# A fused attention and FFN block on one core: another order of the setup work, lighter filler matmuls, and one GpSimd copy moved into the loop

## The reference

```
xn  = layernorm(x)                                # no scale, no shift
qkv = xn @ w_qkv.T + b_qkv                        # per head q, k, v
att = softmax(causal(q k^T / 4 + bias[i - j]))    # position bias per head
a   = (att @ v) @ w_proj.T + b_proj
f   = bf16(fp8(xn) @ fp8(ffn_w)) + ffn_b          # in bf16, two scalar scales
out = x + a + f
```

## Time and profile before

| | |
|---|---|
| median of 3 runs | 779.12 us |
| the 3 runs | 775.78, 779.69, 779.12 us |
| profiled execution, its own time | 775.78 us |
| its span, first to last instruction | 774.0 us |
| mean granted TensorE clock | 0.994 |

### The profile page before, as it was taken

How to read it: one execution, slowest core, us unless ns; L and a number is a source line. 1 busy time by engine, 2 the same in 40 slices (tenths; PEclk the granted TensorE clock), 3 DMA queues, 4 the chain that set the end, 5 groups by cost and what they waited for, 6 DMA issues and landing times.

```text
span 774.0 us, 23381 instructions
## 1 busy us (share of the span) xinstructions
PE 745.4 (96%) x6413; PEld 503.3 (65%) x6413; DVE 634.2 (82%) x2399; ACT 581.6 (75%) x1263; POOL 531.3 (69%) x525
## 2 busy tenths in 40 slices
PE   7989999999999999999999999999999999999997
PEld 4666566666766667676666767666676766667555
DVE  4898798888889888888988888898888889878723
ACT  4457888787788878778877877887787787877672
POOL 8345767686776768776776777677687767767581
PEclk9999999999999999999999999999999999999999
DMA  6432344435334433533543353344335334433301
GB/s 180 178 138 91 121 174 153 126 117 180 121 128 173 151 126 117 182 124 123 173 151 126 118 183 125 119 173 151 129 119 182 127 115 172 152 109 118 120 32 62
DMA packets 55313, 105.67 MB, mean 137 GB/s; under 512 B 10420, under 2 KB 30388, under 8 KB 55284
## 3 DMA queue, kind: packets, MB, share of 16 engines
q1 hardware_dynamic: 53968, 104.52, 37.9%
q10 hardware_dynamic: 1316, 0.80, 0.4%
HBM read 18.42 MB, written 8.90 MB: 35 GB/s over the span
## 4 chain that ended last, share of the span: by engine, by line
PE 76%; DVE 8%; ACT 7%; issue 5%; DMA 1%; DVEq 1%; SPq 1%; POOLq 0%; ACTq 0%; POOL 0%
PE misc_a L673 15%; PE misc_a L557 13%; PE misc_b L557 10%; PE scoreT_b L647 10%; PE scoreT_a L647 5%; PE score_c L624 4%; PE score_a L624 3%; PE misc_b L673 3%; PE misc_b L608 3%; ACT qk_parts L900 2%; PE scoreT_b L650 2%; DVE row_max L1098 2%; DVE qk_parts L1086 1%; PE scoreT_a L650 1%; PE misc_b L600 1%
## 5 line engine op out<-in xcount | busy, mean ns | idle before, releaser
L1316 POOL TENSOR_SCALAR_AFFINE_SELECT probs<-probs 128x512 f32<-128x512 f32 x256 | 160.4, 637 | 194.6 <-ACT probs L1010 191.7
L1098 DVE CUSTOM_DVE_ANT_0 score_b<-score_b,causal_mask_q 128x384 f32<-128x384 f32 (+3 forms) x321 | 162.8, 524 | 90.8 <-PE score_b L624 72.0
L1098 DVE CUSTOM_DVE_ANT_0 score_a<-score_a,causal_mask_q 128x512 f32<-128x512 f32 x319 | 174.8, 564 | 3.7 <-PE score_a L624 3.6
L1098 DVE CUSTOM_DVE_ANT_0 score_c<-score_c,causal_mask_q 128x256 f32<-128x256 f32 (+3 forms) x384 | 172.2, 476 | 0.0
L1010 ACT ACTIVATE probs<-scoreT_b 128x384 f32<-128x384 f32 (+1 forms) x256 | 132.3, 517 | 45.8 <-PE scoreT_b L650 21.6
L1010 ACT ACTIVATE probs<-scoreT_a 128x512 f32<-128x512 f32 (+1 forms) x256 | 143.4, 560 | 9.4 <-PE scoreT_a L650 8.7
L1098 DVE DVE_READ_ACCUMULATOR2_ANT row_max<- 128x1 f32 x1024 | 143.5, 140 | 0.0
L1010 ACT ACTIVATE probs<-scoreT_c 128x384 f32<-128x384 f32 (+1 forms) x256 | 133.9, 523 | 1.4 <-PE scoreT_a L647 0.9
L673 PE MATMUL misc_a<-probs,v_ones 128*32 128x128 f32 (+3 forms) x1536 | 129.5, 440 | 3.6 <-DVE xnT_lo L1080 2.1
L647 PE MATMUL scoreT_b<-stacks 64*128 64x384 f32 (+3 forms) x320 | 120.7, 396 | 1.4 <-ACT probs L1010 1.3
L624 PE MATMUL score_b<-stacks 64*128 64x384 f32 (+3 forms) x321 | 116.0, 393 | 0.0
(11 more groups left out here) (236 smaller groups left out, 1957.3 us busy)
## 6 DMA issues: line engine op xcount, KB each, us to landing
stacks<-qk_parts SPq DMA_DIRECT2D x128, 512.0 KB, 3.7
x_ring<-in_L_attn_x SPq DMA_DIRECT2D x16, 512.0 KB, 3.6
attn<-out_T SPq DMA_DIRECT2D x63, 128.0 KB, 2.6
xn<-recips SPq DMA_DIRECT2D x31, 256.0 KB
out<-x_ring SPq DMA_DIRECT2D x15, 512.0 KB, 3.0
stacks<-neg_max_T SPq DMA_DIRECT2D x128, 4.0 KB
low_features<-neg_max_T SPq DMA_DIRECT2D x126, 4.0 KB
low_features<-probs SPq DMA_DIRECT2D x8, 128.0 KB, 4.3
```

The source lines that it names most:

```text
L1098: last = V.tensor_tensor_reduce(bank, bank, CMQ[:, T - w:T], 1.0, LEAST, ALU.add, ALU.max, MX[:, g % 2, 8 * h + 4 + qt:8 * h + 5 + qt])
L1316: last = GP.affine_select(out=d, in_=d, compare_op=ALU.is_ge, fill=0.0, base=0, pattern=[[0, HU], [1, P]], channel_multiplier=-1)
```

## The change

The setup phase is put in another order, and one POOL step of batch 0 moves. Nothing is computed in another way.

- SP: `load_stack(0, 2)` ahead of `load_low_features(1)`; `send_max` of heads 0 and 1 behind `load_stack(0, 3)`.
- PE: w_proj is transposed ahead of the Q and K projections m = 2, 3, into two banks with one signal each; `job_V(0, 0)` and `job_V(0, 1)` follow chunks n = 2 and n = 4 of the first pass; `project_bias` follows n = 10; the filler is one bf16 matmul of 128 rows by 512 columns (`warm(1, STB[2])`), and six of them ahead of `job_MT(0, 0)`.
- ACT: w_projT high in two halves, behind the V weight.
- DVE: the statistics of batch 1 behind `QK_lo(0, 2)`; `QK_lo(0, 3)` after chunk n = 3 of the first pass; w_projT low in halves after n = 5 and n = 6; the bias is added between the passes.
- POOL: `v_beside_ones(0)` goes from ahead of `body` to behind `quant_write(0)`.

```diff
@@ SP
             sp.wait_ge(const_made, 2)
+            load_stack(0, 2)
             load_low_features(1)
-            sp.wait_ge(mts_ready, 1)
-            send_max(sp, 0, (0, 1))
-            load_stack(0, 2)
...
                 load_stack(b, 3)
+                if first:
+                    sp.wait_ge(mts_ready, 1)
+                    send_max(sp, 0, (0, 1))
@@ PE
             pe.wait_ge(csum_copied, 1)
+            for ct in range(CT):
+                for m in range(2):
+                    last = nc.tensor.transpose(STB[ct][:, P * m:P * m + P], wp_raw[:, m, P * ct:P * ct + P], IDF[:, :])
+                last.then_inc(setup_T, 1)
             for m in (2, 3):
                 job_QK(0, m)
...
-            job_V(0, 0)
             pe.wait_ge(first_pair, 16)
             for n, c in enumerate(FIRST_CHUNKS):
                 if n == CHUNKS // 2:
                     pe.wait_ge(stack_loaded[0], 32)
                 in_turn(scores(0, 0, c, n))
-                if n == 5:
-                    job_V(0, 1)
+                if n in (2, 4):
+                    job_V(0, n // 2 - 1)
+                elif n == 10:
+                    project_bias()
                 else:
-                    warm_halves(1)
-            for ct in range(CT):
...
-            warm_halves(2)
+                    warm(1, STB[2])
+            warm(6, STB[2])
             pe.wait_ge(ident_steps, 8)
             job_MT(0, 0)
...
-                elif c == 8:
-                    project_bias()
                 else:
-                    warm_halves(1)
+                    warm(1, STB[2])
@@ ACT
+            for ct in range(CT):
+                act.wait_ge(setup_T, 4 + ct)
+                A(PH[:, ct, :], STB[ct][:, 0:C], ACT.Copy).then_inc(setup_hi, 1)
             for m in (2, 3):
                 first_QK_evac(m)
...
-            act.wait_ge(setup_T, 4)
-            A(PH[:, :, :], STB[0][:, :].rearrange("p (a c) -> p a c", c=C), ACT.Copy).then_inc(setup_hi, 1)
@@ DVE
-            stats(1, 0)
             QK_lo(0, 0)
-            stats(1, 1)
             QK_lo(0, 1)
-            stats(1, 2)
...
-            stats(1, 3)
             QK_lo(0, 2)
+            for t in range(TT):
+                stats(1, t)
             aggregate(1)
-            QK_lo(0, 3)
...
             for n, c in enumerate(FIRST_CHUNKS):
                 chunk_max(0, 0, c, n)
+                if n == 3:
+                    QK_lo(0, 3)
+                if n in (5, 6):
+                    dve.wait_ge(setup_hi, n - 1)
+                    V.tensor_tensor(PL[:, n - 5, :], STB[n - 5][:, 0:C], PH[:, n - 5, :].bitcast(F32), ALU.subtract) \
+                        .then_inc(setup_lo, 1)
...
+            dve.wait_ge(bp_ready, 1)
+            V.tensor_tensor(BP[:, :], STB[0][:, 0:C], BP[:, :], ALU.add).then_inc(bp_made, 1)
             for c in range(CHUNKS):
                 chunk_max(0, 1, c)
-                if c == 4:
...
-            dve.wait_ge(bp_ready, 1)
-            V.tensor_tensor(BP[:, :], STB[0][:, 0:C], BP[:, :], ALU.add).then_inc(bp_made, 1)
@@ POOL
-            v_beside_ones(0)
...
                     if g == 0:
                         quant_write(b)
-                        if not first:
-                            v_beside_ones(b)
+                        v_beside_ones(b, first)
```

More of the change, by code:

```diff
@@ L725, in project_bias @@
             def project_bias():
-                pe.wait_ge(setup_lo, 4)
+                pe.wait_ge(setup_lo, 5)
                 pe.wait_ge(bq_scaled, 1)
@@ L746, in _ @@
                 in_turn(scores(0, 0, c, n))
-                if n == 5:
-                    job_V(0, 1)
-                else:
-                    warm_halves(1)
-            for ct in range(CT):
[L752 to L755, removed]
-            warm_halves(2)
+                if n in (2, 4):
+                    job_V(0, n // 2 - 1)
+                elif n == 10:
+                    project_bias()
+                else:
+                    warm(1, STB[2])
+            warm(6, STB[2])
             pe.wait_ge(ident_steps, 8)
@@ L1187, in _ @@
                 .then_inc(kq_step, 1)
+            dve.wait_ge(bp_ready, 1)
+            V.tensor_tensor(BP[:, :], STB[0][:, 0:C], BP[:, :], ALU.add).then_inc(bp_made, 1)
             for c in range(CHUNKS):
                 chunk_max(0, 1, c)
-                if c == 4:
-                    dve.wait_ge(setup_hi, 4)
-                    V.tensor_tensor(PL[:, :, :], STB[0][:, :].rearrange("p (a c) -> p a c", c=C), PH[:, :, :].bitcast(F32),
-                                    ALU.subtract).then_inc(setup_lo, 1)
                 if c in (6, 8):
                     T_lo(1, c // 2 - 3)
-            dve.wait_ge(bp_ready, 1)
-            V.tensor_tensor(BP[:, :], STB[0][:, 0:C], BP[:, :], ALU.add).then_inc(bp_made, 1)
             def invert_last(g):
@@ L1336, in add_bias, with v_beside_ones @@
                     .then_inc(xp_ready, 1)
-            def v_beside_ones(b):
-                if isinstance(b, int) and b == 0:
+            def v_beside_ones(b, first):
+                if first:
                     pool.wait_ge(vs_ready, 2)
```

## The result

The changed kernel takes 786.75 us (median of 4 runs, 784.38 to 787.02) against 777.45. Over 27 executions of it, whose median is 785.58 us, the ratio is 1.0104, with a 95% interval of 1.0078 to 1.0131. Run again later beside other kernels it was 1.0084 (1.0053 to 1.0116). So it is slower by some 6 to 9 us, about 1%. I had forecast 2.9 us more than before, and a range that ended at 785.2.

The account below looks back on a forecast made before the run. PE bounds the steady loop and DVE's setup chain sets its entry. DVE's terms (-0.4 + 1.3 + 2.3 - 0.8 - 1.25) give 1.2; plus 2.0 at the product, less 0.3, 2.9 us: 779.12 + 2.9 = 782.0, range 778.3 to 785.2.

Parts of the forecast that it names:

- Start of the pass: DVE's first pass in the setup would begin at 23.85, 0.4 us earlier than 24.24; bounds -0.4 and +0.1.
- job_V(0, 0): PE job of 1.6 us after chunk n = 2; score n = 3 starts near 25.5, so DVE waits 0.5 us.
- job_V(0, 1): PE job after n = 4, held for its bank until QK_lo(0, 3); DVE waits 1.5 us at the sixth chunk.
- project_bias: PE job of 1.9 us after n = 10 of the first pass; DVE waits 1.1 to 1.2 us.
- the bound of 4.2: Upper bound on DVE's first-pass waits, forecast at 3.2 us, if each of the three PE jobs is paid whole.
- Handover and second pass: Between passes 1.67 us as before, with bias addition and six fillers costing nothing; then second pass 8.5 us against 9.28.
- Entry: DVE's first chunk of batch 0 would stand at 45.8, 1.2 us later than 44.62, with no idle ahead.
- POOL copy: In batch 0, copy ends 11.4 us behind DVE's first chunk, at 57.2; PE stands 2.0 us before the product with V.
- The 0.3 of catching up: During PE's wait for the copy, DVE and ACT catch up what they were behind, giving about 0.3 us back.
- The clock: A fall of PE's clock to the 1.2 GHz level costs 1.5 us; chance of one or more 0.30.
- my first rival: Clock falls once, in thinned setup or at the 2 us stand: 4.4 us, so 783.5; once or more, chance 0.30.

Follow-up runs that it names:

- a_halves: Changed kernel with the 64-row filler pairs of the kernel before (both halves of w_proj transposed into one bank); ratio 1.0049 against the kernel before.
- h_qklo: a_halves with QK_lo(0, 3) put back ahead of the first pass; ratio 1.0017 against the kernel before.
- a_again: Changed kernel with no edit, run again for a second profile and ratio; 1.0084 against the kernel before.
- b_pool: Kernel before with only the POOL copy v_beside_ones(0) moved behind quant_write(0); ratio 1.0026 against the kernel before.
- b_h16: Kernel before with its two 64-row fillers kept but in bf16, from the mask tile; ratio 0.9996 against the kernel before.
- b_f128: Kernel before with each pair of 64-row fillers replaced by one float32r filler of 128 rows; ratio 1.0125 against the kernel before.
- b_fill: Kernel before with each pair of 64-row fillers replaced by one bf16 filler of 128 rows; ratio 1.0019 against the kernel before.
- b_none: Kernel before with every warm_halves filler in and between the two passes left out; ratio 1.0080 against the kernel before.

## Why the prediction was wrong

By its own steps:

- **Start of the pass**: 23.85 forecast, 23.61 measured. Right.
- **`job_V(0, 0)`**: wait 0.5 forecast, 1.35 measured. **This is the step that failed**: "n = 3 starts near 25.5". It took the scores as following each other at once, and costed the new filler at nothing, here and in the passes. With a 128-row filler between them they stand 0.7 apart, and n = 3 started at 26.37. With 64-row fillers (`a_halves`) it started at 25.55, as forecast, and the wait is 0.66.
- **`job_V(0, 1)`**: 1.5 forecast, 1.61 measured. The bank, which I gave as the cause, is nearly half of it (`h_qklo`); the rest is the job itself.
- **`project_bias`**: 1.1 to 1.2 forecast; 1.28 with 64-row fillers, 1.56 with the new one. The three waits add up to 4.5 instead of 3.2, above the bound of 4.2: it had each job whole, and nothing for the scores' own spacing.
- **Handover and second pass**: "the six fillers are over before the maxima are ready" was wrong by 0.3 (2.00 against 1.67); the pass took 9.65 instead of 8.5, the filler again.
- **Entry**: 1.2 late forecast, 3.9 measured, 1.3 without the new filler. The mis-sized term is the filler: 0 in the sum, 2.6 to 2.8 us in the runs.
- **POOL copy**: the 11.4 us from DVE's first chunk to its end held (48.55 to 60.04), the stand of 2.0 too. The 0.3 of catching up didn't come: in `a_halves` the lateness goes from 3.42 at the product to 3.57. (In `h_qklo` 0.16 of it came.)
- **The clock**: I gave one fall 1.5 us and 0.30. It costs 1.3 behind the stand and came in both profiles; a second one, in the thin first pass, costs 1.5 in `a_again`. So my first rival was right that a fall comes, but alone it would have given 4.4. What I held against it, 1.6 us of standing at `bp_made` without a fall, was the luck of one profile: in `b_pool` and `b_h16` the clock fell behind that same stand (1.53 and 1.67 us).

Taken along the profile, the 7.30 are 3.93 at the entry (1.31 of it in `a_halves` too, 2.62 the filler), 2.11 more at the product, and 1.26 behind it, the clock. My sum had 1.2, nothing, 2.0 and -0.3 for these. I had looked at the filler only for what it does to the clock. The Trainium skill (TensorEngine Tiling (Array Packing), "Key Properties") has the rule that would have warned me: changing the tiling mode, and not just the tile, drains the array. The runs agree that such a change costs time, here 0.1 to 0.2 us. They do not show that all of it is the draining: in the changed kernel each weight load starts together with its matmul (both at 41.94, the load taking 0.18 us), while before, the load for the score at 35.92 started at 35.69. No run separates the two.

## What to carry to other kernels

A filler matmul is not free because nobody reads it: give it the row shape of the work around it and the half of the array that stands idle, or it can become the bound, as it did here. A job on an in-order engine costs its consumer what exceeds the lead of the buffers, so put long jobs where the lead is whole, or cut them. When a setup step moves into the loop, look for who waits for it there: behind a busy engine it is paid in full, and a stand of PE may be paid a second time in its clock.

## What the hardware showed that I had not expected

- A 512-column matmul of 128 rows between 64-row ones: 0.37 us from a 384-column score to the filler and 0.32 from the filler to the next score (41.94, 42.31, 42.63), where in an unmixed stream the 384 columns take 0.17 (102.80 to 102.97 in `before`) and the 512 of a bf16 filler 0.22 (six of them in 1.46 us at 36.31 in `after`, the last lasting 0.39). So 0.1 to 0.2 us for each change. A pair, score and filler, costs 0.30 more than unmixed with the bf16 filler (0.69 against 0.39). With the float32r filler of `b_f128` it is 0.80, 0.40 more.
- PE shown as 100% busy can still run at the lower clock for 28 us: in the one profile of `b_f128` the granted clock is 0.50 from 28 to 56 us, with PE busy for all of it. In `b_fill`, with a bf16 filler of as many rows, it stays at 1.00.
- Without fillers (`b_none`) the clock from 24 to 60 us is 0.72, and the milestone is 5.9 us late. With the pair of 64-row fillers the clock in the two passes is 1.00 in all nine profiles that have them, and DVE waits in the passes only behind the jobs.
